# Ternary loop of a gated cross-attention and feed-forward kernel: whole numbers as subnormal 16-bit floats, DMA transposes in place of TensorE's

## What is computed

```python
def simple_rms_norm(x):
    d = x.shape[-1]
    n = jnp.linalg.norm(x, axis=-1, keepdims=True)
    return x / jnp.maximum(n, 1e-12) * jnp.sqrt(jnp.asarray(d, x.dtype))
def activation_quant(x):
    scale = 127.0 / jnp.clip(jnp.max(jnp.abs(x), axis=-1, keepdims=True), EPS)
    return jnp.clip(jnp.round(x * scale), -128, 127) / scale
def weight_quant(w):
    scale = 1.0 / jnp.clip(jnp.mean(jnp.abs(w)), EPS)
    return jnp.clip(jnp.round(w * scale), -1, 1) / scale
def bitlinear158(x, w):
    xn = simple_rms_norm(x)
    xq = ste(xn, activation_quant(xn))
    wq = ste(w, weight_quant(w))
    return jnp.einsum('bsi,oi->bso', xq, wq)
...

h = jax.nn.gelu(bitlinear158(x, w1), approximate=False)
h = jax.nn.gelu(h, approximate=False)
return bitlinear158(h, w2)
...
x = x + jnp.tanh(g_ffn[0]) * _L0_ffn_ref(_layernorm(x, axis=-1), L0_ffn_w1, L0_ffn_w2)
```

## Time and profile before

| | |
|---|---|
| three runs, us | 1085.35, 1080.14, 1085.47; median 1085.35 |
| the profiled execution by its own count, us | 1084.0 |
| its span, first to last instruction, us | 1082.3 |
| mean granted TensorE clock, share of full speed | 0.967 |
| busy: TensorE, VectorE, ScalarE, GpSimd, us | 951.2, 721.8, 581.4, 502.1 |
| TensorE weight loads, beside its matmuls, us | 440.1 |

### The profile page before, as it was taken

The page is one execution under the profiler, slowest core; times in us unless marked ns, Lnnn a source line. Parts: engine busy times, 40 slices in busy tenths (PEclk is TensorE's granted clock), DMA queues, the critical chain, the costliest instruction groups (busy, mean ns, idle before and its releaser), DMA issues. The chain is left out here.

```text
span 1082.3 us, 17748 instructions
## 1 busy us (share of the span) xinstructions
PE 951.2 (88%) x5571; PEld 440.1 (41%) x5572; DVE 721.8 (67%) x1419; ACT 581.4 (54%) x881; POOL 502.1 (46%) x539
## 2 busy tenths in 40 slices
PE   0467679999878989999999898998999999899995
PEld 0344344554432322333333223353445555456642
DVE  6988988889867777777776874787344344233348
ACT  5896999998626667667666672533231111111110
POOL 1100334553322577576566661105707887860065
PEclk9987899999997999999999999999999999999998
DMA  9422870000333534332421241996634888956688
GB/s 323 143 78 78 259 227 1 2 1 1 67 99 88 129 75 121 88 83 63 97 63 47 75 80 71 224 356 222 242 106 102 214 210 224 186 134 146 146 302 300
DMA packets 195587, 148.05 MB, mean 137 GB/s; under 512 B 133764, under 2 KB 162436, under 8 KB 195000
## 3 DMA queue, kind: packets, MB, share of 16 engines
q1 hardware_dynamic: 186568, 118.07, 40.9%
q0 software_dynamic: 8080, 27.60, 7.8%
q10 hardware_dynamic: 864, 1.44, 0.5%
HBM read 73.03 MB, written 44.02 MB: 108 GB/s over the span
## 5 line engine op out<-in xcount | busy, mean ns | idle before, releaser
L1857 DVE CUSTOM_DVE_ANT_0 ajunk<-p_row,mask_row 128x512 bf16<-128x512 f32 x256 | 166.2, 686 | 67.9 <-PE p_row L1681 60.1
L1592 ACT ACTIVATE prob<-p_pair,mask_col,any_key 128x512 f32<-128x512 f32 x168 | 121.9, 774 | 65.7 <-PE p_pair L1736 65.2
L1681 PE MATMUL p_row<-ks,early_place 99*128 99x512 f16 x256 | 99.9, 393 | 15.3 <-DVE top L1857 14.7
L1736 PE MATMUL p_pair<-early_place,ks 101*128 101x512 f16 x256 | 97.7, 386 | 5.8 <-ACT prob L1592 4.8
L3039 DVE SCALAR_TENSOR_TENSOR shid<-p_pair,ssilu 128x352 f32<-128x352 f32 x36 | 18.9, 525 | 99.1 <-PE p_pair L2944 99.1
L1592 ACT ACTIVATE early_place<-p_pair,mask_col,any_key 128x512 f32<-128x512 f32 x88 | 64.0, 774 | 29.4 <-PE p_pair L1736 29.2
L2873 ACT ACTIVATE ssilu<-s_gate 128x352 f32<-128x352 f32 x36 | 16.7, 464 | 113.3 <-PE s_gate L2944 113.3
L2959 PE MATMUL s_down<-mw,shT 128*128 (+5 forms) x396 | 75.8, 379 | 0.6 <-DMA shT<-shidr 0.6
L2944 PE MATMUL s_gate<-mw,spare 128*128 (+1 forms) x504 | 68.2, 317 | 4.2 <-DMA spare<-x_slots 4.2
L2861 POOL DMA_INDIRECT mw<-y_slots,dest x32 | 32.4, 1012 | 73.5 <-DMA y_slots<-spare 64.0
L2944 PE MATMUL p_pair<-mw,spare 128*128 (+1 forms) x504 | 66.5, 313 | 0.0
(11 more groups left out here) (459 smaller groups left out, 2284.0 us busy)
## 6 DMA issues: line engine op xcount, KB each, us to landing
x_slots<-nought SPq DMA_DIRECT2D x6, 1536.0 KB, 14.3
y_slots<-spare SPq DMA_DIRECT2D x36, 256.0 KB, 2.2
early_place<-in_ctx SPq DMA_DIRECT2D x8, 1024.0 KB, 6.1
early_place<-halves_d SPq DMA_DIRECT2D x45, 128.0 KB, 2.5
halves_d<-halves SPq DMA_DIRECT2D x18, 256.0 KB, 2.0
x<-in_x SPq DMA_DIRECT2D x4, 1024.0 KB, 7.5
w<-in_L_ffn_w SPq DMA_DIRECT2D x1, 4096.0 KB, 18.3
w<-in_L_ffn_w SPq DMA_DIRECT2D x4, 1024.0 KB, 4.8
```

The lines of the kernel that those rows point to most:

```text
L1592: nc.scalar.activation(prob_of(KB * blk + k, pr)[:, c, :], p_col[c][:], ACT.Exp, bias=mask_col[:, b, k:k + 1], scale=any_key[:, b:b + 1]). ...
L1681: nc.tensor.matmul(p_row[n % 2][:], qs[0:ROWS_R, j, g, t * P:(t + 1) * P], ks[b % 2][0:ROWS_R, g, :], start=True, stop=True).then_inc(t_ro ...
L1736: nc.tensor.matmul(p_col[c][:], ks[b % 2][0:ROWS_C, g, k * P:(k + 1) * P], qs[0:ROWS_C, j, g, :], start=True, stop=True).then_inc(t_col, 1)
L1857: nc.vector.tensor_tensor_reduce(junk[:, n % 2, :], p_row[n % 2][:], mask_row[:, blk // HPG, :], 1.0, -3e38, ALU.add, ALU.max, top[blk % 2 ...
```

## The change

Whole numbers are now subnormal 16-bit floats: the quantising multiplies by `TINY` = 2^-24, the step of the subnormals, so that writing 16 bits rounds to a whole number of steps, and the scale of the result is divided by it. Both weights are f16 in place of bf16. Nothing has to be subtracted, so nothing has to pass through PSUM: SyncE turns the quantised rows by DMA transposes straight to where TensorE reads them. For product one that is two transposes of 128 x 256 a tile (`turn_in`, now SyncE's), eight of them one after the other for a group of four; for product two, two of 128 x 1024 a tile (`turn_hidden`, SyncE's). TensorE's transposes and the evictions of ScalarE and VectorE go. The products two take turns in two PSUM banks `po`, so the addition may be two tiles behind. The pieces for the next stage are spread differently over steps 10 to 15, and the transposes for it are issued from within the loop, those of the context at t = 12, those of x at t = 14.

```diff
-LIFT = 1536.0
-LIFTED = ROUND + 0x6600
+TINY = 2.0 ** -24
...
-    w1T = sb(st, "w1T", [P, KB, INNER], BF16)
-    w2T = sb(st, "w2T", [P, IB, D], BF16)
+    w1T = sb(st, "w1T", [P, KB, INNER], F16)
+    w2T = sb(st, "w2T", [P, IB, D], F16)
...
-    q1 = [low_half(t[:]) for t in y]
-    q1T = sb(st, "q1T", [P, KB, P], BF16)
+    q1, q1T = ([t.rearrange("p t (h c) -> p t h c", h=2)[:, :, :, n * P:(n + 1) * P].bitcast(F16) for t in (y[0][:], y[1])] for n in range(2))
...
-    q2 = [low_half(t) for t in h]
+    q2 = [t.rearrange("p (h c) -> p h c", h=2)[:, :, 0:HALF // 2].bitcast(F16) for t in h]
...
+            def turn_in(t):
+
+                sp.wait_ge(b_q1, t + 1)
+                need(sp, b_turn1[t % QUARTET], 32 * (t // QUARTET))
+                g, i = t // QUARTET % 2, t % QUARTET
+                for n in range(2):
+                    sp.dma_start_transpose(q1T[g][:, i, n, :].rearrange("p (k n) -> p k n", n=P), q1[g][:, i, n, :]).then_inc(b_turn1[i], 16)
+
+            def turn_hidden(t):
+
+                sp.wait_ge(b_q2, t + 1)
+                if t < 2:
+                    sp.wait_ge(s_prod, PRODUCTS - TPB)
+                need(sp, b_prod2, t - 1)
+                for n in range(2):
+                    sp.dma_start_transpose(q2T[t % 2][:, n * IB // 2:(n + 1) * IB // 2, :], q2[t % 3][:, n, :]
+                                           ).then_inc(b_turn2[t % 2], 16)
+
+            for t in range(*GROUPS_OF[0]):
+                turn_in(t)
+            for t in range(*GROUPS_OF[1]):
+                turn_in(t)
+            for t in range(NT + 1):
+                if t >= 1:
+                    turn_hidden(t - 1)
+                if AHEAD.get(t, (None,))[0] == 3:
+                    for i in range(*GROUPS_OF[AHEAD[t][1]]):
+                        turn_in(i)
+                if t == NT - 4:
+                    sp.wait_ge(s_prod, PRODUCTS)
+                    sp.wait_ge(b_ctxrows, 2)
+                    for i in range(TPB):
+                        early.turn(sp, early.ctxT, first_ctx, i, early.t_ct)
+                if t == NT - 2:
+                    sp.wait_ge(b_xrows, 2)
+                    for i in range(TPB):
+                        early.turn(sp, early.xT, keep, i, early.t_xt)
...
             def product_hidden(t):
-                need(pe, b_added, t)
+                need(pe, b_added, t - 1)
+                pe.wait_ge(b_turn2[t % 2], 32 * (t // 2 + 1))
                 for k in range(IB):
-                    if k % (IB // 2) == 0:
-                        pe.wait_ge(b_evac2[2 * k // IB], t + 1)
-                    mm = nc.tensor.matmul(py[:], q2T[t % 2][:, k, :], w2T[:, k, :], start=(k == 0), stop=(k == IB - 1))
+                    mm = nc.tensor.matmul(po[t % 2][:], q2T[t % 2][:, k, :], w2T[:, k, :], start=(k == 0), stop=(k == IB - 1))
...
-                nc.vector.tensor_scalar(ht, ht, k2[:, t:t + 1], LIFTED, ALU.mult, ALU.add).then_inc(b_q2, 1)
+                nc.vector.tensor_scalar(q2[t % 3], h[t % 3].rearrange("p (h c) -> p h c", h=2), k2[:, t:t + 1], TINY, ALU.mult, ALU.mult).then_inc(b_q2, 1)
...
-                if t == 9:
-                    next_statistics()
                 if t == 10:
                     first_statistics()
+                    next_statistics(0)
                 if t == 11:
                     first_variances()
                     context_high()
+                    context_low(0)
                 if t == 12:
+                    context_low(TPB // 2)
                     first_values()
                 if t == 13:
                     rows_high()
                     rows_low(0)
+                    next_statistics(1)
                 if t == 14:
                     rows_low(TPB // 2)
-                    context_low(0)
+                    kv_high()
+                    next_statistics(2, 3)
                 if t == 15:
-                    context_low(TPB // 2)
-                    kv_high()
+                    next_variances()
```

More of the change, by code:

```diff
@@ L228, in stage_cross_ternary @@
     TURNED, EVICTED, RESIDUALS, PRODUCTS, WEIGHTS, SCALED = 2 * KB * B, 2 * KB * B, TPB * B, TPB * B, WG, 2 * B
[L230 to L234, removed]
+    b_zero, b_clear, b_pool, b_dve, b_mv, b_r1, b_y, b_ymax, b_k1, b_q1, b_prod1 = (
+        sem("b_" + n) for n in ("zero", "clear", "pool", "dve", "mv", "r1", "y", "ymax", "k1", "q1", "prod1"))
+    b_gelu1, b_gelu2, b_hsq, b_hmax, b_k2, b_a2, b_q2, b_prod2, b_added, b_gate = (
+        sem("b_" + n) for n in ("gelu1", "gelu2", "hsq", "hmax", "k2", "a2", "q2", "prod2", "added", "gate"))
+    b_turn1, b_turn2 = ([sem(f"b_turn{m}_{n}") for n in range(count)] for m, count in ((1, QUARTET), (2, 2)))
     b_xv, b_xr, b_ctxrows, b_xrows = (sem("b_" + n) for n in ("xv", "xr", "ctxrows", "xrows"))
@@ L240, in stage_cross_ternary, with columns_of @@
     AHEAD = {(a - 6 + n): (n, g) for g, (a, b) in enumerate(GROUPS_OF) if g > 1 for n in range(4)}
+    def columns_of(t):
+        return [q1T[t // QUARTET % 2][:, t % QUARTET, k // 2, k % 2 * P:(k % 2 + 1) * P] for k in range(KB)]
     with nc.Block() as block:
@@ L568, in turn_w @@
                     mm.then_inc(s_wT, 1)
[L570 to L575 removed]
             def product_in(t, n):
                 if n == 0:
[L579 removed]
+                    pe.wait_ge(b_turn1[t % QUARTET], 32 * (t // QUARTET + 1))
                 need(pe, b_gelu1, 2 * (t - 1) + n + 1)
@@ L659, in _ @@
                         product_in(t + 1, n)
-                    if t == 1 and n == 0:
-                        pe.wait_ge(s_added, RESIDUALS)
-                    if t >= 1:
-                        turn_hidden(t - 1, n)
-                if t + 2 < NT:
-                    turn_in(t + 2)
                 if t == 0:
                     product(3, 3)
+                if t == 1:
+                    pe.wait_ge(s_added, RESIDUALS)
                 if t >= 1:
                     product_hidden(t - 1)
-            for n in range(2):
-                turn_hidden(NT - 1, n)
             product_hidden(NT - 1)
@@ L675, in _ @@
         def _(dve):
-            dve.wait_ge(s_const, 10)
+            dve.wait_ge(s_const, 9)
             link = Chain(dve, s_dve)
@@ L872, in rows_low, with next_statistics, next_variances @@
                 nc.vector.tensor_tensor(keep[:, c, D:2 * D], val_x[1][:, c, :], keep[:, c, 0:D], ALU.subtract).then_inc(b_xrows, 1)
-            def next_statistics():
+            def next_statistics(*tiles):
                 dve.wait_ge(b_added, 2 * TPB)
-                for k in range(TPB):
+                for k in tiles:
                     blink(nc.vector.bn_stats(early.stats[:, k, :], x[:, TPB + k, :]))
+            def next_variances():
                 nc.vector.memset(pause[:], 0.0)
```

85 lines of the change are left out of this document (15 added, 70 removed).

## The result

The changed kernel takes 1109.0 us, the median of four runs from 1107.5 to 1114.3, where the kernel before takes 1083.6: a ratio of 1.0258, 95% interval 1.0219 to 1.0298. It is slower, as forecast, but by 25.4 us and not by 14.8, one microsecond beyond the range.

What follows compares the result with a forecast made beforehand. TensorE bounds the kernel before; the two-tile loop through DMA transposes binds after. 175.4 + 100.8 + 18.9 + 3.8 + 12.1 + 6.8 = 317.8 us against 303.0, hence 1098.8 us; 8-in-10 range 1077 to 1108.

Steps and rivals of the forecast that it cites:

- the odd chain: Loop from one odd tile's maximum to the maximum two tiles on, through DMA transposes and addition: 14.4 us, the bound.
- that rival: Quantising, writing two separate 16-bit halves, takes 2.28 us for 1.28 in each of 8 passes: +8, 1107 us; chance 0.06.
- The rivals that made the kernel faster: Loop fits under TensorE, 1066.8 us, chance 0.05; small input transposes cheap, s near 0.5, 1079.3 us, chance 0.16.
- the last rival: Hidden transposes land late, 5.2 us, 1.9 more in each of 8 passes: +15, 1114 us; chance 0.04.
- three stretched rounds: Odd-chain rounds from tiles 1, 5 and 9, where SyncE's eight input transposes precede the hidden pair: near 21 us, 22.5 with clock.
- the end: From the last maximum to the last addition: 12.1 us, with a further clock loss of 1.7 once at the end.
- I take s = 1.1: SyncE's time in us per 128 by 256 input transpose; eight add 6.3 us to each of three rounds, 18.9 in all.
- each costs 1.7 on the chain: Lowered TensorE clock after long idle times, in three stretched rounds and once at the end: 1.7 us each, 6.8 in all.
- every round would pay: By the skill page's rule on DMA waits, the clock falls in plain rounds too: four more, 6.8 us more; not expected.
- 0.17, three steps 1.45, 0.03: From a tile's maximum to its quantising: hand-off to GpSimd 0.17, its three scale steps 1.45, hand-off 0.03 us.
- 1.0 us by my reckoning of the two queues: Four context transposes issued at tile 12 push product two of tile 12 ahead of tile 13's: 1.0 us.
- the gain on offer: With TensorE still the bound, 14 tiles between the second maximum and the last take 96.6 us in place of 114.9.

Runs made afterwards that it cites:

- e1: Changed kernel with the input transposes issued two per tile behind each hidden pair, not eight in a row; ratio 1.0036 to the kernel before, about 1087.5 us.
- e10: Kernel of e9 with each tile's hidden values turned by four transposes of 128x512 in place of two of 128x1024; ratio 1.0054, 1088.0 us.
- e5: Changed kernel with 34 unused matmuls ahead of product two of tiles 1, 5 and 9, keeping TensorE busy; ratio 1.0168, about 1102 us.
- e9: Kernel of e4 with the eight next-stage transposes moved behind the hidden pairs of the last tiles; ratio 0.9935, 1075.1 us.
- e4: Changed kernel with e1's spread input transposes and VectorE's addition behind the maximum; ratio 0.9993, on another chip 0.9968 (1079.2 us).
- e2: Changed kernel with the eight input transposes kept together but issued one hidden pair later, ahead of tiles 2, 6 and 10; ratio 1.023, about 1108.5 us.
- e6: Kernel before with only the subnormal 16-bit number format, TensorE's transposes and the old order kept; ratio 0.9991.

## Why the prediction came out as it did

**The mechanism held.** The four things it named are in the rows: the odd chain binds up to the maximum of tile 13, the eights stand ahead of the pairs of tiles 1, 5 and 9, the DMA ends TensorE's waits, and quantising keeps its rate (1.29 us in L793, against the 2.28 of that rival). The rivals that made the kernel faster needed cheap small transposes or no queue; e1 shows that without the block the loss would indeed be gone, and the rows that the block is there. The late landings of the last rival didn't come either: 3.2 to 3.9 us.

**The sum, term by term**, on the profiled times, from the end of tile 1's maximum to the end of the last addition:

| term | forecast us | measured us |
|---|---|---|
| end of tile 1's maximum | 175.4 | 173.7 |
| three stretched rounds | 3 x 22.4 = 67.2 | 75.5 |
| two plain rounds, tiles 3 to 5 and 7 to 9 | 28.8 | 30.4 |
| round 11 to 13 | 15.7 | 15.6 |
| round 13 to 15 | 16.9 | 19.2 |
| the end | 13.8 | 13.7 |
| end of the last addition | 317.8 | 328.1 |

The miss of 10.3 us is 8.3 in the stretched rounds, 1.6 in the plain ones and 2.3 in the last, less 1.7 at the start and 0.2 in the two others. Four terms were too small: the queue (6.6 us), the clock behind it (1.8), the scale steps of the plain rounds, and the last round. The start, which I cost at nothing, came 1.7 earlier: VectorE's weights let product one of tile 0 go at 155.34 and not at 157.87. In e1, which has the same code up to there, it is 158.01, so that is not the change's doing.

*The queue, step "I take s = 1.1".* Line 274 of the changed kernel as a single line, and its landing:

```profile
L274 SPq DMA_TRANSPOSE keep<-keep x16: 1170/1244/2196, 150.3 to 225.2; - x16
L274 SPq DMA_TRANSPOSE xT<-xT x16: 1168/1246/2128, 174.2 to 265.7; - x16
...
DMA to landing us min/median/max: 2.3/2.4/4.6
```

The median is 1.24 us for 128x256, about the 1.21 of 128x768 in the earlier trace rows. The eights take 11.1, 11.6 and 10.3 where I had 8.8: 2.3, 2.8 and 1.5 us too little, 6.6 in all. In the third no issue is long: its eight take 10.30 us because each starts 1.29 after the one before, 1.24 and a gap of 0.05. That alone is 1.5 of each eight, and it is above the flat end of 1.21 that I had set. The rest, 0.8 and 1.3 us, is one issue of 2.13 and one of 2.20 us in the first two eights, and a gap of 0.5 in the second. Each row has its most beside the median (2.35, 3.04 and 3.90 us), and a term that is multiplied by eight should have carried it. I also let the price fall with the width, where the rows were flat. TensorE's idle time ahead of the three products was 8.0 to 9.1 us where I had 5 to 6. The Trainium skill ("DMA: Bandwidth & Descriptors", "Why a DMA increments its semaphore by 16 and not by 1") gives earlier generations one push per tile for a transpose from SBUF, by which a quarter of the tiles would cost about a quarter. SyncE's 1.24 us for 128x256 beside 1.30 for 128x1024, and e10's 5.12 for 2.61, don't bear that out.

*The clock, "each costs 1.7 on the chain".* I priced a return from 2.59 us without work. After 8 to 9 us without it the whole product ran low: 6.47 and 6.34 for 3.62, so 2.9 and 2.7 us, and 4.91 in the third, 1.3. Two of the three were a microsecond too little and one 0.4 too much. e5 shows the share on its own, 7.4 us of three rounds. In the plain rounds, with waits of 0.9 to 1.6 us in the changed kernel and up to 1.82 in e9, product two stays at 3.61. The Trainium skill ("TensorE: Matmul & The Clock Gate", "HAM oscillation — how this bites in real kernels") tells that waits for DMA make the clock fall again and again in a kernel whose groups of products are shorter than the wait behind them. The long waits here agree with it. The plain rounds, with 13.8 us of products to 0.9 to 1.6 of waiting, are not such a case, and the prediction's "every round would pay" read the page too widely.

*The plain rounds, "0.17, three steps 1.45, 0.03".* From the end of tile 3's maximum to its quantising VectorE's rows above give 2.4 us where I had 1.65. GpSimd's timeline in the changed kernel:

```profile
199.74 0.77 POOL L382 TENSOR_SCALAR b_clip<-b_hmax,b_r 128x1 f32<-128x1 f32 x1 [9.07 <-DVE b_hmax L951]
200.66 0.77 POOL L383 TENSOR_TENSOR b_inv<-b_clip,neg_ones 128x1 f32<-128x1 f32 x1
201.62 0.27 POOL L384 TENSOR_SCALAR b_k<-b_inv,b_r 128x1 f32<-128x1 f32 x1 [0.19 <-POOL b_inv L383]
```

The three steps take 2.15 us (199.74 to 201.89) where the earlier trace rows has 1.45, the first of them 0.77 for 0.30; they run beside the normalising L770, 1.91 us of VectorE from 199.49. I had read a tile in which a maximum stood beside them (L792 of the kernel before, from 233.86). In the round from 7 to 9 one of the pair landed after 3.9 us and not 3.3, which is another 0.5.

*The last round, "1.0 us by my reckoning of the two queues".* The four context transposes took 6.23 us, from 288.04, ahead of a pair whose values were ready at 291.3 and that went out at 294.37: 3.0 us, and the product behind it took 4.91 us for 3.62, 1.3 more. Product one of tile 15 and product two of tile 13 stand behind that one on TensorE, so here the even tile held up the odd one. The prediction had 1.0 us for this; it did not carry the queue through the even tile and its clock. e9 shows what it was worth: 3.1 us of the loop.

*The end was right by luck.* 13.7 us for 13.8, but not on the path that I had added up. TensorE in the changed kernel, the last two products in one row:

```profile
318.34 8.96 PE L593 MATMUL po<-w2T,ctxT 128*128 128x512 f16 x32 [7.46 <-DMA ctxT<-w]
```

Tile 14's pair went out behind the four transposes of x, at 313.60. Its product waited 7.46 us and took 5.34 of the 8.96, at a granted clock of 0.64 (window 318.3 to 323.7). Tile 15's own pair, issued by 318.65 and with 3.3 us to land, was there by about 322.0; its product began at 323.68, behind tile 14's, and ran at full clock. The 1.7 us of clock that I had put on the last product was paid by the one before it.

**Where the gain on offer went.** The prediction had seven rounds of 14.4 us without the eights, 100.8 for 114.9, and 3.8 more for the last ones. That sum failed too, though the eights hid it: with the queue cut up and nothing else changed (e1) the rounds take 113.2, 8.6 more than 104.6, in the main by GpSimd's arithmetic in two rounds (17.0 and 16.3 us) and by the transposes for the next stage in the last (19.6). Most of the gain came only with two changes of order that the change doesn't have, the addition behind the maximum (e4) and the late transposes for the next stage (e9): the rounds take 105.3 and the loop falls from 137.4 to 127.3, 10.1 us. The first maximum stands 1.5 later, and 7.4 us reach the time.

## What to carry to other kernels

When work moves from an engine to DMA, write down the issuing queue in order, with what waits for each entry: a block of prefetches ahead of one transfer that is waited for costs its length less the room that this transfer had, every time (8.0 to 9.1 us of idle TensorE for blocks of 10.3 to 11.6 us here), and moving the block mostly moves the wait (6.0 to 6.2 us in e2). Cut such a block into pieces that fit between the waited-for ones, and do the same for the transfers of the next stage. A long wait of TensorE costs the clock as well, on the same chain, so it is to be priced from rows with as long an idle time, and from more than one, since idle times of 2.5 to 3.9 us went either way here.

## What the runs showed of the hardware that was not expected

- SyncE's time for a DMA transpose of 16-bit elements hardly depends on its width: 1.24 us for 128x256, 1.27 for 128x512, 1.30 for 128x1024. The landing does somewhat: 2.4, 2.5 and 3.3 us in the median. Of the changed kernel's 72 transposes in the loop three took 2.13 to 2.20 us on SyncE; in e2, e9 and e10 no input transpose (128x256) took more than 1.38. What makes the long ones is open.
- Two GpSimd steps on a single column take 0.77 us each beside VectorE's normalising of f32 tiles (L770), 0.30 and 0.56 beside a maximum, and 1.13 and 1.36 in tile 13, beside the work for the next stage. That the two engines get into each other's way there is only argued; no run took one away.
- Subnormal 16-bit floats, written by VectorE and read by TensorE and by the copies out of PSUM, cost nothing that can be measured (e6, 0.9961 to 1.0021).
- The length of one idle time does not settle TensorE's clock. Product two took 4.91 us after 3.37 (changed kernel), 5.03 after 3.89 (e9) and 5.30 after 2.46 (tile 12 in e5), but 3.61 after 3.75 (e4 again). The first half of product one of tile 0 took 1.90 us after 2.84 (kernel before) and 3.31 after 2.71 (e9).
- Chips differ: the kernel before took 1115.0 us beside e1 to e4, 1082.3 and 1082.5 beside the others. e4 took 1116.0 on the first and 1079.2 on another, with loops of 132.1 and 130.4; behind the loop the profiled executions have 815.4 us (1114.7 - 299.32) and 772.2 (1070.0 - 297.77). e4's ratio was 0.9993 on the one and 0.9968 on the other, within each other's intervals; the times are not to be compared.
